# Scan of a PReLU recurrence: VectorE's work on chunks 2 and 3 in the order sloped, sloped, state, state

## What is computed

```
Wc = conv_w[:, :, 0, 4]                       # 512 x 512
def step(prev, x_i):                          # prev: 4 images x 512 channels x 16
    y = einsum('oc,nch->noh', Wc, prev) + conv_b
    y = where(y >= 0, y, prelu_a * y)
    cur = y + x_i
    return cur, cur
_, fwd_rest = scan(step, x[0], x[1:])                 # 15 steps forward
fl = concatenate([x[0:1], fwd_rest])
_, bwd_rest = scan(step, fl[-1], fl[:-1], reverse=True)   # 15 steps back
```

## Time and profile before

| | |
|---|---|
| median of 3 runs | 281.69 us |
| the profiled execution | 282.56 us, span 280.8 us |
| TensorE matmuls busy | 269.4 us (96%) |
| TensorE weight loads busy | 228.4 us (81%) |
| VectorE busy | 173.5 us (62%) |
| ScalarE busy | 99.3 us (35%) |
| GpSimd busy | 64.8 us (23%) |
| granted TensorE clock | full (9 of 9 in all 40 slices) |
| first scan's steady part | 81.6 to 148.6 us of the span |

### The profile page before, as it was taken

The page is one execution under the profiler, slowest core; times in us unless marked ns, Lnnn a source line. Parts: engine busy times, 40 slices in busy tenths (PEclk is TensorE's granted clock), DMA queues, the critical chain, the costliest instruction groups (busy, mean ns, idle before and its releaser), DMA issues.

```text
span 280.8 us, 11061 instructions
## 1 busy us (share of the span) xinstructions
PE 269.4 (96%) x4539; PEld 228.4 (81%) x4539; DVE 173.5 (62%) x634; ACT 99.3 (35%) x229; POOL 64.8 (23%) x94
## 2 busy tenths in 40 slices
PE   6999999999979999999999999999999999999996
PEld 2488888888478888888885688878786699999996
DVE  2685464555657777777777866464567455555553
ACT  2054554545643333333330337646457400000000
POOL 0109300004222222233331130000012433334432
PEclk9999999999999999999999999999999999999999
DMA  7980000000000000000000000000000000002222
GB/s 227 413 349 5 1 0 2 1 0 0 0 5 4 0 0 0 0 0 0 0 0 1 0 0 2 1 1 0 2 0 0 2 0 0 0 8 68 75 75 75
DMA packets 4479, 9.25 MB, mean 33 GB/s; under 512 B 624, under 2 KB 3056, under 8 KB 3952
## 3 DMA queue, kind: packets, MB, share of 16 engines
q1 hardware_dynamic: 4176, 8.53, 8.3%
q10 hardware_dynamic: 288, 0.52, 0.5%
HBM read 6.96 MB, written 2.10 MB: 32 GB/s over the span
## 4 chain that ended last, share of the span: by engine, by line
PE 66%; DVE 23%; ACT 4%; issue 3%; DMA 2%; POOL 1%; DVEq 0%; ACTq 0%; POOLq 0%
PE banks L377 25%; PE banks L298 19%; DVE state L717 10%; DVE sloped L712 9%; PE banks L354 6%; PE banks L310 5%; PE banks L270 4%; PE banks L317 2%; ACT xn L455 2%; PE banks L329 2%; DMA x<-in_x 2%; DVE st L543 1%; PE banks L279 1%; PE banks L345 1%; ACT rel L468 1%
## 5 line engine op out<-in xcount | busy, mean ns | idle before, releaser
L377 PE MATMUL banks<-state,wc 128*64 128x64 f32 x3840 | 126.0, 224 | 3.3 <-DVE state L717 1.5
L377 PEld LDWEIGHTS banks<-state,wc 128*64 128x64 f32 x3840 | 119.2, 138 | 10.3 <-DVE state L717 5.8
L298 PE MATMUL banks<-xn,w 128*128 128x256 f32 x256 | 60.9, 383 | 0.0
L298 PEld LDWEIGHTS banks<-xn,w 128*128 128x128 f32 x256 | 46.5, 190 | 6.5 <-issue 1.3
L695 DVE SCALAR_TENSOR_TENSOR state<-banks,negb,inb 128x64 f32<-128x64 f32 x116 | 29.3, 282 | 25.3 <-PE banks L377 23.8
L832 POOL TENSOR_TENSOR rstd<-gvar,mhalf 128x4 f32<-128x4 f32 (+1 forms) x8 | 14.6, 1827 | 123.4 <-DVE gvar L576 123.4
L712 DVE SCALAR_TENSOR_TENSOR sloped<-banks,par,share 128x64 f32<-128x64 f32 x116 | 30.1, 280 | 14.8 <-PE banks L377 14.8
L354 PE MATMUL banks<-probT,xnT 128*128 128x256 f32 x128 | 29.5, 381 | 0.8 <-ACT rel L468 0.8
L717 DVE SCALAR_TENSOR_TENSOR state<-sloped,bent,banks 128x64 f32<-128x64 f32 x112 | 28.8, 278 | 2.0
L354 PEld LDWEIGHTS banks<-probT,xnT 128*128 128x128 f32 x128 | 24.2, 190 | 4.8 <-ACT rel L468 1.6
L498 ACT COPY banks<-inb 128x256 f32 (+1 forms) x29 | 10.9, 376 | 44.4 <-DVE state L717 42.0
(11 more groups left out here) (76 smaller groups left out, 211.8 us busy)
## 6 DMA issues: line engine op xcount, KB each, us to landing
w<-in_w SPq DMA_DIRECT2D x2, 1024.0 KB, 10.7
wc<-in_wc SPq DMA_DIRECT2D x2, 1024.0 KB, 13.9
result<-xh SPq DMA_DIRECT2D x15, 128.0 KB, 1.8
x<-in_x SPq DMA_DIRECT2D x3, 512.0 KB, 9.0
x<-in_x ACTq DMA_DIRECT2D x1, 256.0 KB, 4.6
x<-in_x SPq DMA_DIRECT2D x1, 256.0 KB, 4.4
w<-in_w ACTq DMA_DIRECT2D x1, 256.0 KB, 5.0
w<-in_w SPq DMA_DIRECT2D x1, 256.0 KB, 12.2
```

What stands on the lines that cost most here:

```text
L298: mm = nc.tensor.matmul(bank[2 + m // 2][:, m % 2 * POS:(m % 2 + 1) * POS], w3[l][:, k, m * P:(m + 1) * P], xn_s[:, k], start=(k == 0), st ...
L377: mm = nc.tensor.matmul(bank[K * h + m][c:c + TILE, 0:COLS], wc[l][:, k, m * P + c:m * P + c + TILE], state[:, h, k], start=first and not ...
```

## The change

In `prelu_step`, chunks 2 and 3 get the order that chunks 0 and 1 have: both sloped branches, then both states. This holds for all 30 steps, the first included. The instructions are the same ones with the same waits.

```diff
-                    prelu_sloped(q, t, h, 0)
-                    prelu_sloped(q, t, h, 1)
-                    prelu_state(q, t, h, 0)
-                    prelu_state(q, t, h, 1)
-                    for k in range(2, K):
-                        prelu_sloped(q, t, h, k)
-                        prelu_state(q, t, h, k)
+                    for ks in (range(K // 2), range(K // 2, K)):
+                        for k in ks:
+                            prelu_sloped(q, t, h, k)
+                        for k in ks:
+                            prelu_state(q, t, h, k)
```

## The result

The changed kernel takes 275.10 us (median of 4 runs, 274.79 to 276.16), against 281.73 us of the kernel before in the same comparison. The ratio is 0.9778, with a 95% interval from 0.9759 to 0.9797: 6.6 us less. Predicted were 275.6 us, in a range from 275.0 to 277.2, and 6.1 us less.

What follows compares the result with a forecast made beforehand. The prediction took a loop between TensorE and VectorE in the first scan as the bound. Savings of 5.74 + 0.21 + 0.13 = 6.1 us off 281.69 gave 275.6 us, range 275.0 to 277.2.

Steps and rivals of the forecast that it cites:

- The loop: First scan: TensorE's products 0, VectorE's eight instructions and the handover of state 3 make up the whole 2.39 us step.
- Sloped 3 doesn't wait: First scan, VectorE: products 3 are there before sloped 3's new place, with 0.06 to 0.13 us to spare.
- State 2 is late next: First scan: the state-2 point comes 0.07 us later and is on the path; state 3 is no longer waited for.
- The step: First scan: 2.18 us against 2.39, a gain of 0.205 us a step, 5.7 us (5.5 to 6.0) over 28 steps.
- The range: Whole kernel: 275.0 us (step's rounding and all 0.25 us at the end) to 277.2 us (rival 2, rival 1's begin).
- rival 1: First scan: products 3 are late, sloped 3 waits; with 0.1 us beyond the spare, 278.5 us; chance 8%.
- Step 0: First step of the first scan: products already summed, state-3 point at 81.39 and not 81.61; 0.2 us gained.
- The end: Behind the first scan: 12 matmuls on zeros ahead of the group sums let 0.13 of 0.25 us count.
- The rule against it: VectorE: the skill's pipe-drain rule, read as making order worth nothing, so the time stays 281.7 us.
- 4: First scan: state 2 held behind the wait for products 3; with a notice of 0.40 us, 282.5 us; chance 2%.
- Rival 2: First scan: a hitch at the state-3 point, up to 0.05 us a step, 277.0 us; chance 6%.
- Rival 3: First scan: the 0.32 us distance belongs to chunk 2 or 3, not dependence; step stays 2.39, 281.7 us; chance 4%.

Runs made afterwards that it cites:

- the edit of the share wait: Wait for ScalarE's share placed behind the wait for products 0: on the changed kernel 272.71 us, on the kernel before 279.21 us.
- the experiments that delayed state 2 by 0.32 and 0.26 us: Two edits of the changed kernel: state 3 ahead of state 2, 284.53 us; chunks 0 and 1 one after the other, 282.85 us.
- the three other orders of the same eight instructions: Edits of the changed kernel: state 3 before state 2, 284.53 us; chunks 0 and 1 unpaired, 282.85 us; all sloped branches before all states, 289.09 us.
- the order with the first pair apart: Changed kernel with chunks 0 and 1 one after the other (sloped 0, state 0, sloped 1, state 1), chunks 2 and 3 paired: 282.85 us.

## Why the prediction was right, point by point

**The loop.** That the step was VectorE's chain from products 0 to state 3, and not the busy share of any engine, is shown by the edit of the share wait: 0.07 us off the notice of products 0 came off the step, before and after the change, but in the steps with a third wait.

**Sloped 3 doesn't wait.** Right: no idle time stands before it. The notice took 0.05 us (with all sloped branches first), and the spare was some 0.1 us.

**State 2 is late next.** Right: the state-2 point stands 0.05 us behind the end of state 2, and the experiments that delayed state 2 by 0.32 and 0.26 us moved the step by as much.

**The step.** Predicted 2.18, measured 2.177 in the mean, against 2.39. The term of the sum, 5.7 us (5.5 to 6.0), was mis-sized: it measured 6.0, as I took 0.205 a step and the records give 0.215 (the prediction's own 2.39 and 2.18 differ by 0.21). The error is that of rows rounded to 0.01 us, ten of them in one sum and times 28. Two points 28 steps apart gave the old step to 0.001; for the new one there was no such pair of points.

**The range.** Its low end is 0.2 us lower than its terms: 6.0 + 0.2 + 0.25 us off 281.69 is 275.2, and not 275.0. The measured 275.10 lies 0.1 us beyond what the terms allow, and is inside the stated range only by that slip. What the terms measured, 6.0 + 0.2 + 0.2 off 281.7, is 275.2 to 275.3; the rest is of the size by which two series of the changed kernel differ (275.10 and 275.26). In rival 1, too, 0.1 us beyond the spare makes 278.4 and not 278.5.

**Step 0.** Predicted 0.21, measured 0.22.

**The end.** The step of the prediction that failed: "TensorE must first run the 12 matmuls on zeros", so that 0.13 of the 0.25 us count. Measured are 0.23. I had set the start of the sums' weight load against the first free place of a matmul. In the trace the load doesn't wait for that place: it starts at 144.69, 0.05 us behind the statistics, while the matmuls on zeros run until 145.00. Only the first matmul of the sums waits for them, 0.14 us behind its load where it was 0.00 before; the second starts 0.03 us behind its own load in both traces. So the two matmuls, which started 0.13 us apart before, now start 0.03 apart. The kernel with one matmul less shows that only 0.02 to 0.03 us were left to gain (one execution, by its trace).

**The rule against it.** The prediction quotes half of what the section says. The sentence "the next op does not start until the 8-stage pipe empties" (the Trainium skill, "VectorE: DVE Perf Modes", section "The DRAIN you can't avoid") is followed there by "A next op that is not held starts earlier". So the section doesn't say that order is worth nothing, and it was wrong to take it for a forecast of 281.7 us. The rows agree with its second sentence: an instruction that doesn't need the one in front starts 0.19 to 0.20 us behind it, though each lasts 0.28, and one that needs it 0.31 to 0.32 behind. By the first sentence alone, the three other orders of the same eight instructions would be equal on VectorE, but for waits on other engines; the order with the first pair apart has all of its 0.26 us from VectorE's own distances.

**The rivals.** Rival 1 and 4 are a real mechanism and come at the price that was worked out, when an order puts all states behind products 3; in this order there was room. Rival 2, a hitch with 0.04 us to spare, didn't come. Rival 3 is excluded by the first pair. What is left of the 6.6 us beyond these terms, 0.1 to 0.2, lies within what the start of an execution varies.

## What to carry to other kernels

In a recurrence handed between two engines, write the step down as a loop of starts, handovers and distances, and ask of each edit what it does to the length of that loop and which handover is late next. With VectorE instructions as short as these (0.28 us each), put one independent instruction between a producer and its consumer, but only one whose own input is there when its turn comes: sloped 3 had 0.1 us to spare in the changed kernel, and with all sloped branches first it held up every state. And where an instruction waits for two things, don't write the one that is satisfied last as the last, so that it sits on the instruction itself, and look whether a wait holds up work that doesn't need it (share and the four sums of step 0).

## What the runs showed that I had not expected

- The order of two waits on one instruction is worth 0.07 us in each step that has two: products' end to start 0.12 us with the late wait as an instruction of its own, 0.05 with it on the instruction.
- The start of the kernel doesn't always run at the same pace: the same 11 matmuls on zeros take between 2.5 and 4.65 us in the twelve traces, with the same instructions ahead of them. The windows from 8 to 16 us, of the kernel before and of the changed one, both give the granted clock as 1.00, its upper level of 2.4 GHz, but 33 matmuls in one and 44 in the other:

```profile
8.00:16.00 8.00, 8.00 (x33) 4.83 (x32) 5.73 (x21) 0.87 (x2) 1.23 (x2) 1.00 1.03 419
```
```profile
8.00:16.00 8.00, 8.00 (x44) 5.45 (x44) 6.05 (x23) 2.46 (x5) 1.23 (x2) 1.00 1.03 415
```

  Where the column and the pace disagree, the pace is what the time follows. What decides it wasn't tried.
- A chain of waits in which VectorE's lines of this scan (L712, L717) fell from 19% to none belongs to a kernel whose step was still set by VectorE's state 2, by a wait of 0.2 us a step that no idle row shows.
